# One ring of four banks for both kinds of score product, in an attention kernel with hand-drawn orders

## The reference, cut to what matters

```
qn  = layer_norm(x)   * g_q  + b_q;    kvn = layer_norm(ctx) * g_kv + b_kv
Q, K, V = qn @ Wq, kvn @ Wk, kvn @ Wv           # split in 16 heads
attn = softmax(Q @ K^T / sqrt(32))              # over the 512 keys
out  = x + gelu((attn @ V) @ Wo + bo)           # exact gelu
```

## Time and profile before

| | us |
|---|---|
| median of three runs | 3539.74 (3538.9 to 3542.51) |
| profiled execution, its own time | 3541.05 |
| span of that execution, first to last instruction | 3539.0 |
| TensorE busy | 3405.7 (96%) |
| ScalarE, GpSimd, VectorE busy | 2356.9, 2314.2, 2302.9 |

### The profile page before, as it was taken

The page is one execution under the profiler, slowest core; times in us unless marked ns, Lnnn a source line. Parts: engine busy times, 40 slices in busy tenths (PEclk is TensorE's granted clock), DMA queues, the critical chain, the costliest instruction groups (busy, mean ns, idle before and its releaser), DMA issues.

```text
span 3539.0 us, 60544 instructions
## 1 busy us (share of the span) xinstructions
PE 3405.7 (96%) x16611; PEld 2122.4 (60%) x16611; DVE 2302.9 (65%) x4775; ACT 2356.9 (67%) x3982; POOL 2314.2 (65%) x1547
## 2 busy tenths in 40 slices
PE   7999999999999999999999999999999999999998
PEld 5566565666655665656666656656566666566564
DVE  6666666676566666666765666666667656666664
ACT  4576666766666766667666667666676666676665
POOL 2657667667667576676576675766765766756654
PEclk9999999999999999999999999999999999999999
DMA  5456566456555565664565555556645655555553
GB/s 131 68 93 106 98 104 102 79 92 112 101 98 86 92 104 98 104 105 75 92 114 103 95 87 92 102 100 103 108 74 92 113 102 95 88 92 101 101 80 65
DMA packets 186492, 340.15 MB, mean 96 GB/s; under 512 B 20561, under 2 KB 20577, under 8 KB 186466
## 3 DMA queue, kind: packets, MB, share of 16 engines
q1 hardware_dynamic: 186432, 339.82, 56.0%
q10 hardware_dynamic: 34, 0.01, 0.0%
HBM read 104.87 MB, written 33.55 MB: 39 GB/s over the span
## 4 chain that ended last, share of the span: by engine, by line
PE 82%; ACT 8%; DVE 5%; issue 4%; POOL 0%; DMA 0%; ACTq 0%; DVEq 0%; SPq 0%; POOLq 0%
PE gen L759 33%; PE score L779 15%; PE score L787 14%; PE ctx L802 13%; ACT q_stack L540 4%; PE gen L848 3%; PE gen L814 3%; DVE maxes L625 2%; ACT L495 1%; ACT ctx_hl L501 1%; ACT probs L495 1%; DVE q_nat L608 1%; ACT max_cut L536 1%; ACT q_nat L526 1%; DVE gen L666 1%
## 5 line engine op out<-in xcount | busy, mean ns | idle before, releaser
L419 POOL TENSOR_TENSOR probs<-probs 128x1024 f32<-128x1024 f32 x762 | 1803.8, 2394 | 500.9 <-PE ctx L802 497.3
L625 DVE TENSOR_REDUCE maxes<-score 128x1 f32<-128x512 f32 x2048 | 1345.4, 683 | 263.7 <-PE score L787 241.3
L495 ACT ACTIVATE probs<-score 128x512 f32<-128x512 f32 x2048 | 1143.4, 601 | 308.5 <-PE score L779 282.0
L779 PE MATMUL score<-q_stack,k_stack 128*128 128x512 f32 x2048 | 818.5, 430 | 23.6 <-ACT probs L495 15.1
L787 PE MATMUL score<-k_stack,q_stack 96*128 96x512 f32 x2048 | 817.1, 428 | 16.5 <-DVE maxes L625 9.7
L779 PEld LDWEIGHTS score<-q_stack,k_stack 128*128 128x128 f32 x2048 | 376.1, 189 | 358.5 <-ACT probs L495 200.2
L787 PEld LDWEIGHTS score<-k_stack,q_stack 96*128 96x128 f32 x2048 | 384.0, 189 | 286.1 <-DVE maxes L625 191.3
L802 PE MATMUL ctx<-probs,v_sb 128*32 128x512 f32 x4096 | 487.1, 599 | 0.5 <-ACT probs L495 0.5
L759 PE MATMUL gen<-w_v,cT 128*128 128x512 f32 x1536 | 422.9, 397 | 13.3 <-DVE q_nat L608 13.3
L434 POOL TENSOR_TENSOR rstd<-var_eps,minus_half 128x1 f32<-128x1 f32 x256 | 141.1, 551 | 428.3 <-DVE neg_mean L656 428.2
L759 PE MATMUL gen<-cT,w_k 128*128 128x512 f32 x1536 | 409.9, 396 | 3.9 <-DVE w_k L564 3.0
(11 more groups left out here) (85 smaller groups left out, 2744.3 us busy)
## 6 DMA issues: line engine op xcount, KB each, us to landing
k_stack<-k_nat SPq DMA_DIRECT2D x384, 256.0 KB, 7.7
q_stack<-q_nat SPq DMA_DIRECT2D x384, 256.0 KB, 5.6
tok<-in_x SPq DMA_DIRECT2D x132, 256.0 KB, 10.5
tok<-in_ctx SPq DMA_DIRECT2D x128, 256.0 KB, 11.1
res<-in_x SPq DMA_DIRECT2D x124, 256.0 KB, 6.6
out<-res SPq DMA_DIRECT2D x124, 256.0 KB, 2.5
probs<-in_L_xattn_Wq SPq DMA_DIRECT2D x1, 1024.0 KB, 8.4
probs<-in_L_xattn_Wk SPq DMA_DIRECT2D x1, 1024.0 KB, 10.6
```

What stands on the lines that cost most here:

```text
L419: pool.tensor_tensor(probs[:, c + 1, heads], probs[:, c + 1, heads], probs[:, c, heads], ALU.add).then_inc(pool_added, 1)
L495: act.activation(probs[:, n, part, :], score[i % 2][:], ACT.Exp, scale=SCALE).then_inc(exp_done, 1)
L625: dve.tensor_reduce(maxes[:, u1 % 2, SROW + i:SROW + i + 1], score[2 + i % 2][:], AX_X, ALU.max, negate=True).then_inc(max_done, 1)
L779: pe.matmul(score[i % 2][:, :], k_stack[:, s % 2, part, P * n:P * (n + 1)], q_stack[:, s % 2, part, :], start=True, stop=True).then_inc(st ...
```

## The change

Both kinds of score take the four banks in turn, in the order in which they stand in TensorE's list: SCORE_AT gives each its number in that order, and score_bank waits for whichever reader belongs to the score four back. The readers take the same bank by score_at. All orders are drawn up anew. In the last step the first two output tiles go to a ctx bank and a gen bank instead of score banks. At the start ScalarE scales the key weights itself, so that GpSimd has the query's four tiles only, and the first unit's query copies are issued from ScalarE's queue, two of the three as soon as the high half is there.

```diff
     "pe": (
-        "q*3 z st*2 v s st s st v s st*2 s v st s st s v s st*2 s v st s*2 st v st s st s st s st s pv s*2 pv m "
-        "k*3 o*2",
-        "st*2 o st*2 q st q*2 k st k st*2 k st x st s*2 pv s st*2 z st s x s st x st s st s x*2 pv s x s x s*2 x "
-        "o*2 s*2 o s o s o s o m o*3",
-        "k st s*2 k s st s st s st k st s st s z st s*2 st*2 s st s st s st s st s st*2 s*2 st pv*2 m q*3",
-        "k st*2 k st*2 k st q st*2 q st q st*2 pv st*2 z st s*2 st*2 s st s*2 pv s*2 v s*2 v s*2 v s*2 v s*2 v s "
-        "v m",
+        "q*3 z st*4 v*2 st*2 s v s*2 st*2 v s st*2 s v s st s*2 v st s st s st s st s st s*4 pv*2 m k*3 o*3",
+        "st*2 q st*2 q st q st k*2 st*2 k x st*2 s st pv s*3 z st x s st*2 s x st x st s*3 x pv x*2 s*4 x o*4 s o "
+        "s*2 o m o*2",
+        "o k st*2 k s*2 k st*2 s st z st*2 s st s st s st s st s st s st s st*2 s st s*5 pv*2 m q*3",
+        "k*2 st*3 k q st*2 q st*3 q st*4 pv z s st*4 s*2 v s pv s*4 v s*2 v s*3 v s*2 v s v m",
     ),
     "act": (
-        "q st*10 norm v st*6 v split mh mx*3 k mx",
-        "norm st*4 gelu st*2 q st*2 x st norm k st norm st norm st*2 x st x st*2 x norm x norm*2 x*3 gelu*2 mh "
-        "mx*4 split",
-        "gelu st*5 k st*11 mh split mx*4 q",
-        "st*6 k st*6 q st*4 v*2 mh split mx*4",
+        "q st*6 split st*2 v st*3 norm st*5 v mh mx*3 k mx norm*2",
+        "st*2 gelu st*2 q st*4 x norm st k st norm st norm st x st*2 x st*2 x norm x norm x*3 gelu*2 mh mx*4 "
+        "split",
+        "gelu st*2 k st*14 split mh mx*3 q mx",
+        "st*8 k st*4 q st*4 v split v mh mx*4",
     ),
     "dve": (
-        "q zt s*2 ln s*2 zr la ln lv s*2 zb s*3 la lv s*4 cn ln s*2 la s md ln lv ln ml la*2 k ob",
-        "lv ln lv ln la*2 q s x s k lv s ln zt s*2 x*2 lv zr s la lv x s x s*2 x*2 s zb s x s*2 ob s*3 ob md cn "
+        "q zt zr zb cn ln s ln s*2 ln la*2 s lv s la s*3 lv s*4 ln la s lv s*2 lv s md ml k ln",
+        "ln ob la ln q la lv ln s lv x la lv k la s*3 zt s x lv s x s*2 zr x*2 s zb x*2 s cn x s*2 ob s*4 ob md "
         "ml ob",
-        "s*7 k s*7 zt s*2 zr zb cn md ml q",
-        "k zt s*3 zr q s*2 zb s*11 md cn ml",
+        "s*2 k s zt s zr s*9 zb s*2 cn s md ml q",
+        "k s q zt zr s*2 zb cn s*13 md ml",
     ),
     "pool": (
-        "ln*2 add split add ln add*2 res_add add*2",
-        "ln*2 add*2 ln*3 add res_add add res_add add*2 split",
-        "add*6 split",
-        "add res_add add*5 split",
+        "ln*2 split ln add*5 res_add ln*2 add",
+        "ln*3 add*4 res_add*2 add split add",
+        "res_add add*6 split",
+        "add*5 split add",
     ),
     "sp": (
-        "load*8 rq rk store",
-        "res rq rk store",
-        "rk store rq",
-        "first_res res store rq rk first_res",
+        "load*7 rq load rk store res",
+        "rk rq store res store*2",
+        "first_res rk rq",
+        "first_res rq rk",
     ),
...
+SCORES = [[(_kind, HU * _n + _part) for _kind, _n, _part in PLAN["pe"][_s] if _kind in ("st", "s")] for _s in range(NU)]
+SCORE_AT = {(_s, *_item): _i for _s in range(NU) for _i, _item in enumerate(SCORES[_s])}
+PER_STEP = 2 * NC * HU
...
+        def score_at(s, kind, i):
+            return score[SCORE_AT[(s, kind, i)] % NC]
+
+        def score_bank(eng, b, s, kind, i):
+            back = PER_STEP * s + SCORE_AT[(s, kind, i)] - NC
+            while back > -2 * PER_STEP * NU:
+                b2, s2 = b + back // (PER_STEP * NU), back % (PER_STEP * NU) // PER_STEP
+                kind2, i2 = SCORES[s2][back % PER_STEP]
+                b3, u3 = unit(b2, s2, 0 if kind2 == "st" else 1)
+                if valid(b3):
+                    wait(eng, exp_done if kind2 == "st" else max_done, 16 * (NU * b3 + u3) + i2 + 1)
+                    break
+                back -= NC
+            return score_at(s, kind, i)
...
-                    for n, (name, gain) in enumerate((("q", 0), ("k", 2))):
-                        pool.wait_ge(w_loaded[name], 16)
-                        pool.wait_ge(full["x"], NC)
-                        for c in range(NC):
-                            pool.tensor_scalar(by_dim(name, scaled(name, c)), by_head(name, probs[:, n, c, :]),
-                                               norm_cols[:, gain, c:c + 1], None, ALU.mult).then_inc(w_scaled, 1)
+                    pool.wait_ge(w_loaded["q"], 16)
+                    for c in range(NC):
+                        pool.tensor_scalar(by_dim("q", scaled("q", c)), by_head("q", probs[:, 0, c, :]),
+                                           norm_cols[:, 0, c:c + 1], None, ALU.mult).then_inc(q_scaled, 1)
...
+                    act.wait_ge(w_loaded["k"], 16)
+                    act.wait_ge(full["x"], NC)
+                    for c in range(NC):
+                        act.activation(by_dim("k", scaled("k", c)), by_head("k", probs[:, 1, c, :]), ACT.Identity,
+                                       scale=norm_cols[:, 2, c:c + 1]).then_inc(k_scaled, 1)
                     high_weights(0, "q", 0)
                     high_weights(1, "k", 2)
...
+                            if known(b) and (b, s) == (-1, 2):
+                                act.wait_ge(q_hi, 1)
+                                act.wait_ge(stack_used, 1)
+                                restack(act, u2, q_nat, q_stack, (0, 0), q_stacked)
+                                act.wait_ge(free["q"], 1)
+                                act.dma_start(raw(q_stack[2 * DH:3 * DH, u2 % 2, :, :]),
+                                              raw(q_nat[:, 1, :])).then_inc(q_stacked, 16)
...
-                            wait(pe, exp_done, 16 * t + i - 1)
-                            pe.matmul(score[i % 2][:, :], k_stack[:, s % 2, part, P * n:P * (n + 1)],
+                            pe.matmul(score_bank(pe, b, s, "st", i)[:, :], k_stack[:, s % 2, part, P * n:P * (n + 1)],
                                       q_stack[:, s % 2, part, :], start=True, stop=True).then_inc(st_full, 1)
...
-                            wait(pe, max_done, 16 * t1 + i - 1)
-                            pe.matmul(score[2 + i % 2][:, :], q_stack[0:KROWS, u1 % 2, n, P * part:P * (part + 1)],
+                            pe.matmul(score_bank(pe, b, s, "s", i)[:, :], q_stack[0:KROWS, u1 % 2, n, P * part:P * (part + 1)],
                                       k_stack[0:KROWS, u1 % 2, n, :], start=True, stop=True).then_inc(s_full, 1)
                         if (kind, n) == ("pv", 1) and last(b) and s == NU - 1:
-                            wait(pe, max_done, 16 * NU * B)
+                            wait(pe, ctx_read, NU * B - 1)
                             wait(pe, ctx_split, NU * B - 2)
-                            last_products((0, 1), (0, 1))
+                            last_products((0,), (0, 1))
+                            for kind2, count in (("z", NU * B - 1), ("m", NU * B), ("q", NU * B), ("k", NU * B),
+                                                 ("x", 2 * NC * B), ("v", NC * B), ("o", NC * (B - 1))):
+                                wait(pe, free[kind2], count)
+                            last_products((1,), (0, 1))
```

33 lines of the change are left out of this document (18 added, 15 removed).

## The result

The changed kernel takes 3455.44 us (median of 4 runs, 3452.61 to 3455.83), the kernel before in the same comparison 3540.75 us (4 runs, 3538.9 to 3542.51). The ratio is 0.9757, with a 95% interval of 0.9741 to 0.9774. The direction was forecast.

A forecast was written before the change was run, and what follows sets the result against it. TensorE's instruction stream, with waits hidden in its busy time, was taken to bound the kernel. From 3541.05 us, 37 (loop), 5 (start) and 2 (end) came off: 3497 us, with 8 in 10 between 3462 and 3535.

The forecast's parts named there:

- -1.2 us a batch: Rounded sum over the loop's four stretches; times 31 periods it gave -37 us, bounds -93 and 0.
- A: Loop stretch ending at step 3's m (transpose of the maxima): 0.8 us shorter, from 28.83 to 28.0.
- B: Loop stretch ending at step 0's m (transpose of the maxima): 0.35 us shorter, mainly by losing v's wait.
- C: Loop stretch ending at step 1's m: net -0.1 us, about 0.5 gained in front, stalls at three x products.
- D: Loop stretch ending at step 2's m: 0 change, held by the chain to the first exponential and ScalarE's work.
- The start: Before the loop: -5 us in all, from scaling the key on ScalarE and overlapping the first 16 reductions better.
- -3.0 for the key scaling: At the start: key scaling on ScalarE brings the first key product to 31.3 instead of 34.3 us.
- The end: Last step's lone transposed scores: five pairs go from 1.54 to about 1.1 to 1.2 us, -2 us.
- (1): Rival on the loop: ring only renames waits, since every stretch ends on a chain; 3534 us, chance 0.14.
- (2): Rival on the loop: 0.1 us late loads vanish in B, C and A too; 3456 us, chance 0.10.
- (3): Rival, slower: GpSimd's last addition comes late for step 2's z; 3553 us if 2 us over, chance 0.11.
- (4): Rival on TensorE's clock: it falls for part of each batch; 3600 us or more, chance 0.01.

The follow-up runs named there:

- ring_old_orders: Changed kernel with all order strings of the kernel before, keeping the shared four-bank ring and the start edits; 3548.07 us, ratio to before 1.0028.
- pv_z_apart: Changed kernel with one plain score put between pv and z in TensorE's step 3; 3464.8 us, ratio to before 0.9786.
- two_then_v: Changed kernel with two transposed scores, not four, ahead of the first v part in TensorE's step 0; 3467.22 us, ratio to before 0.9791.
- pv_apart: Changed kernel with two plain scores put between the two pv products of TensorE's step 0; 3461.43 us, ratio to before 0.9772.
- old_step2: Changed kernel with step 2's earlier orders of TensorE, ScalarE and VectorE; 3467.35 us, ratio to before 0.98.
- key_on_gpsimd: Changed kernel with the key weights scaled by GpSimd behind the query's again; 3453.35 us, ratio to before 0.975.
- query_from_sync: Changed kernel with the first unit's query copies issued from SyncE's queue behind the key's again; 3453.59 us, ratio to before 0.9758.
- old_step3: Changed kernel with step 3's earlier orders of TensorE, ScalarE and VectorE, GpSimd's kept new; 3559.74 us, ratio to before 1.0052.
- old_step3_kept_split: Changed kernel with step 3's earlier orders except ScalarE's split, and step 2's query copy behind all four shift copies; 3520.61 us, ratio to before 0.9938.
- early_plain: Changed kernel with two plain scores ahead of step 3's first pv and the last v parts together; 3585.84 us, ratio to before 1.0127.
- new_orders_two_rings: Changed kernel with two banks for each score kind again and one step 1 reduction moved ahead of the last x; 4218.28 us, ratio 1.1917.

## Why the prediction was wrong in its size

The step that failed is the sum "-1.2 us a batch": its terms were mis-sized, three of them too small and one too large. It measured -2.58, so -80 us instead of -37. What the walk put at nothing was the late loads at pairs between value products (A), the earlier low half of the query (B), the stalls that the old order already had at its x products (C), and the ring's own price (D). By stretch:

- **A, forecast -0.8, measured -1.27.** The prediction said that "the ring helps where one kind stands in a row" and looked for long rows only. A pair of one kind between value products is already too long for two banks when the next pair comes before both are read: 0.51 us in four rounds (ring_old_orders), in a stretch that the walk had at full pace. Then pv beside z, taken with fewer alternating scores at 0.4 for both, is worth 0.37 alone (pv_z_apart). The front had the right size: from m to the first pv 11.16 us before and 11.33 after, with two scores (0.47) more in it, so 0.30 where 0.25 was forecast. These make 1.18, and 0.27 are given back in a longer wait at m (0.42 against 0.15); the 0.36 between that and 1.27 isn't taken apart.
- **B, forecast -0.35, measured -0.81.** The v wait was seen at half its size. From m to the end of z, six scores and two v parts it is 8.61 us before and 7.81 after: 0.80, so nearly all of B's gain is at its head. The order of v and scores is 0.38 of it (two_then_v), as forecast. But the query's low half, for which v waits, is itself ready earlier: it starts 4.92 us after m before and 4.50 after (rows below), since ScalarE's split now stands ahead of m's chain in step 3 instead of inside it. The walk left this out. The two pv's next to each other were not counted either, 0.20 (pv_apart), although the price of a switch stood in the prediction; the rest of B, from there to m, lasts as long as before (14.26 against 14.23 us), so the new order gives those 0.20 back elsewhere.

VectorE's low half of the query, before (m at 1043.66) and after (m at 910.16):

```profile
1048.58 0.75 DVE L608 SCALAR_TENSOR_TENSOR q_nat<-gen,bias_q,q_nat 128x512 fp32r<-128x512 f32 x1 [3.49 <-ACT q_nat L526]
```

```profile
914.66 0.75 DVE L637 SCALAR_TENSOR_TENSOR q_nat<-gen,bias_q,q_nat 128x512 fp32r<-128x512 f32 x1 [3.33 <-ACT q_nat L548]
```

- **C, forecast -0.1, measured -0.80.** The gain at the front was right: from m to the first pv, with as many scores and parts in both orders, 1081.41 - 1066.50 = 14.91 us before and 946.80 - 932.23 = 14.57 after, 0.34 less where 0.5 was forecast. But that was to be eaten by stalls of 0.3 to 0.4 at the x products. Such stalls are there: one score takes 0.55 us until the next x (952.84 to 953.39) and four scores 1.30 (958.05 to 959.35), 0.3 to 0.4 more than their work each. What the walk left out is that the old order had larger ones: two x take 1.29 us until pv (from 1088.14) where the work is 0.72, and two scores 1.26 until the last x (from 1092.66) where it is 0.47. So from the first pv to the last x both take 12.5 us (12.51 before, 12.55 after), and the new order does two scores more in it, 0.47 us of work. Behind the last x those two scores are missing and the rest is the chain that was described, with 0.98 us of wait at m as against 0.95 before: nothing gained. With the old orders the ring makes C 0.16 longer, so all of the 0.80 depends on the new ones; no run changes a single item of C's front or middle, so which item it is stays open.

The rows of C, before and then after:

```profile
1081.41 1.92 PE L802 MATMUL ctx<-probs,v_sb 128*32 128x512 f32 x16
...
1088.14 1.36 PE L848 MATMUL gen<-ident,tok 128*128 128x128 f32 x8
...
1092.66 1.09 PE L787 MATMUL score<-k_stack,q_stack 96*128 96x512 f32 x2
1093.92 0.65 PE L848 MATMUL gen<-ident,tok 128*128 128x128 f32 x4 [0.17 <-DVE cT L606]
```

```profile
946.80 1.92 PE L833 MATMUL ctx<-probs,v_sb 128*32 128x512 f32 x16
...
952.84 0.48 PE L807 MATMUL score<-q_stack,k_stack 128*128 128x512 f32 x1
...
958.05 1.17 PE L814 MATMUL score<-k_stack,q_stack 96*128 96x512 f32 x4
959.35 0.65 PE L879 MATMUL gen<-ident,tok 128*128 128x128 f32 x4
...
967.32 0.30 PE L899 MATMUL gen<-ident,maxes 128*128 128x128 f32 x1 [0.98 <-DVE maxes L713]
```

- **D, forecast 0, measured +0.29.** The chain from m to the first exponential was right (the exponential starts 973.77 - 967.32 = 6.45 us after m, before 1108.85 - 1102.39 = 6.46). What was missed is that a single ring makes plain scores queue behind it: +0.86, of which the new order takes 0.57 back (old_step2). The prediction named only the ring's help, never a loss.

The start, forecast -5, measured -4.9, is right by accident. Its largest term, -3.0 for the key scaling, is 0 (key_on_gpsimd). ScalarE's scaling was priced at the 2.55 us of the value weights and took 4.11; and even on GpSimd's price the bias turn, which I had left where it was, stands in front of the key product. The term "-2" for the first reductions measured -2.6, and the rest, 2.8, came within batch 0, outside what its shorter period explains: 2.3 of it between batch 0's second and third m (35.06 us before, 31.92 after), where ring_old_orders has 32.43, so most of it needs no new orders. No term of the forecast stood for that. The copies were rightly given nothing. The Trainium skill (DMA: Bandwidth & Descriptors, Issuing engines are not separate DMA queues) says that only issue time is saved by another queue, and query_from_sync agrees: first score at 55.3 against 55.43 us. The end, forecast -2, gave -1.7 behind the last m, 1.6 of it up to the first pv behind the lone transposed scores; the mechanism and the size were right. The other 1.5 of the 3.2 are the last batch's B, C and D.

Of the rivals, (1) has one true part: the stretches do end on their chains, and the m wait grew to 46.0 us. But TensorE reached them by more than it lost there. (2) had the size, 3456, but its condition, that the late loads vanish, is not what happened: 254.1 of 358.5 us of idle remain, and part of the gain (the switches, 0.20 and 0.22 a batch) has nothing to do with them. That its number fits is luck. Much of the gain was in places that I had walked as free of stall. (3) didn't happen in the changed kernel, and did in old_step3, at 1.7 us a batch: the mechanism was real, and the new order avoids it by ScalarE's early split (with the split put back there, in old_step3_kept_split, z waits 7.2 us in all instead of 53.2). (4) did not come up in the changed kernel, whose clock is 1.00 in all four windows. The Trainium skill (TensorE: Matmul & The Clock Gate, A second HAM failure mode: psum-queue depth-cycling) warns of cycling through banks with small idles; here a ring of four cycled without it. In the loop the clock fell in two kernels, early_plain and new_orders_two_rings, with idles of 2.30 and 2.39 us in the windows shown.
